# Output weights' lower parts on another engine, sums in pieces, loads spread over slots, and part of the first batch's keys and values among the preparation

## The chip, the cores and the metric

The kernel runs on one core of a Trainium2 chip. The metric is the time of one execution on the device in microseconds, median of several runs. In the profile the engines are PE (TensorE), PEld (its weight loads), DVE (VectorE), ACT (ScalarE), POOL (GpSimd) and SP (SyncE, which here issues every DMA).

## What is computed

Two attention layers over x and a context, both (32, 128, 1024) in float32, outputs the same shape. Cut to what matters:

```python
# layer 0, per batch: 8 heads of 16 rows, attention among the rows
q = Wq @ y + bq;  k = Wk @ y + bk;  v = Wv @ x + bv
attn = softmax(q k^T / sqrt(128))            # per head 16 x 16
o = Wo @ (attn v) + bo + x
h = norm_over_rows_and_columns(o) * gn_w[:, None] + gn_b[:, None]
# layer 1: 32 query heads of 32, 8 key heads, low-rank additions on every weight
lin(x, W, A, B) = x @ W + 2 * (x @ A @ B)
q = lin(h, Wq, Aq, Bq); k = lin(ctx, Wk, Ak, Bk); v = lin(ctx, Wv, Av, Bv)
attn = softmax(q k^T / sqrt(32))             # per head 128 x 128
out = h + lin(attn v, Wo, Ao, Bo)
```

## The kernel before

Every engine runs a program written out by hand; semaphores alone set the order between them, and each engine does its instructions strictly in its own order. Matrices are split in a rounded part and a rest ("hi" and "lo", type fp32r), and a product is three matmuls: hi x hi, hi x lo, lo x hi.

*Preparation.* The low-rank factors are merged into the key and value weights in eight units: `prep_product(n)` on TensorE, `prep_merge(n)` on VectorE, the high part on ScalarE, the low part on GpSimd (even n) or VectorE (odd n). `turn_layer0()` transposes the small weights of layer 0 behind unit 5.

*Batches.* For each of the 32 batches TensorE does the Gram matrix of y, the keys and values of layer 1 (`kv_products(b, chunks)`, eight chunks of 128 rows with three matmuls each, bank 2), and between these chunks the short chain of layer 0: `t1_product`, `score_product`, `n1_product`, `mix_product`, `mixed_x`. The result h goes to memory (h_dram). The output weights, merged with their factors, go to wo_dram as four blocks.

*Slots.* Then follows one loop over slots w = 0 to 511, the same on all engines. In slots 0 to 255 (QUERY_SLOTS is 256) TensorE projects queries, six matmuls a slot (`project_first`, `project_q`, L642); `split_q` on VectorE splits them, and `put_q` on SyncE writes them to q_dram every eight slots, 3 x 512 KB. `turn_h` transposes h in slots 0 to 26 and on, from h_in tiles that `load_h` brings. `scores(n)` (L697) takes a k_stack and a q_stack tile; VectorE makes their `maxima` and `negs` (L1190, L1195), ScalarE the `exponents` (L941), of which only the sums are kept. From slot 237 on one `scores_again(n)` a slot (L729) makes the scores a second time, transposed and with the logarithm of the sum subtracted, ScalarE makes the `probabilities` (probT, L958) and `context(k)` (L740) multiplies with the values.

In slots 256 to 511 TensorE projects the outputs: 16 pairs of batches of 16 slots each, with seven products per pair of 2x2 blocks in place of eight (`project_o`, L679). For these the four blocks of the output weights (w_blk, 1 MB each) are loaded by `load_wo` in the slots of WO_LOADS; GpSimd makes four differences of blocks (`out_weights`); ScalarE makes the high part of each of the seven weights in the slots of WO_PARTS (`out_hi`, L853), and GpSimd the low part (`out_lo`, L1458). Product m of pair 0 waits for `wo_lo` to reach m + 1. The weights' places are those of wq and hT, so each step also waits for a count of `q_mm`, the query projections done. VectorE splits the seven left operands (`split_op`, `combine`) and adds the products into the output blocks (`add_out`).

A score unit n has its slot in score_slot; its query load stands in slot 8 * queries_out + 10 at the earliest (score_load_at), its keys load in score_keys_at. again_load_at and again_rows_at place the loads of the second pass. SyncE works its slots in order too: a load that waits (for written queries in `wait_queries`, for a buffer) holds all behind it.

Order within a slot. TensorE: scores, product, transposes, context, scores_again. ScalarE: probabilities and context of the slot before, `keep_product`, `out_hi`, exponents. VectorE: maxima, transposed h, `split_q`, then from slot 256 the combinations, splits and sums.

## Time and profile before

| what | value |
|---|---|
| median of 3 runs | 1410.39 us (1408.95 to 1411.84) |
| the profiled execution's own time | 1413.77 us |
| its span, first to last instruction | 1412.0 us |
| mean granted clock of TensorE | 0.987 |
| busy: TensorE, VectorE, ScalarE, GpSimd | 1350.5, 935.0, 824.1, 190.4 us |
| exponents L941, mean of one | 343 ns, 1024 of them |
| probabilities L958, mean of one | 603 ns, 256 of them |
| high part of an output weight L853, mean of one | 1.9 us, 7 of them |

The page lists busy time per engine; waits are found in the views of waits and in the time lines, where a bracket behind a row gives the idle time before it and what ended it. Batches last from about 30 to 425 us, the query slots to 926.8 us, the pairs of output slots to the end.

### The profile page before, as it was taken

The numbers are of one execution on the slowest core, as the hardware profiler recorded it, in microseconds if no ns is written. First come the engines' busy times: TensorE is split into PE (matmuls) and PEld (weight loads), VectorE is DVE, ScalarE is ACT, GpSimd is POOL, SyncE is SP. The second block draws the span as 40 slices with busy tenths as digits, with TensorE's granted clock in tenths as the row PEclk, the third lists the DMA queues.
The fourth block names the chain that finished last, engine by engine and source line by source line (L and its number), as shares of the span: only waits on it lengthen the run. The fifth ranks groups of instructions, "written<-read, shape, count | busy, mean of one in ns | idle before, by whom it ended". The sixth has DMA issues, their size and how long they took to land.

```text
span 1412.0 us, 24026 instructions
## 1 busy us (share of the span) xinstructions
PE 1350.5 (96%) x7135; PEld 1062.1 (75%) x7135; DVE 935.0 (66%) x2061; ACT 824.1 (58%) x2924; POOL 190.4 (13%) x124
## 2 busy tenths in 40 slices
PE   6999999999989999999999997979999999999998
PEld 5777788787778788888888886656776676676666
DVE  5666666666555577777777774586766777766665
ACT  4556665555530677777757774556666666665440
POOL 5533332222210000000000002650000000000000
PEclk9999999999999999999999999999999999999999
DMA  6455556666747688888888889876988889877762
GB/s 177 143 196 202 201 200 203 224 220 224 249 151 225 226 260 266 258 254 263 254 252 262 253 253 289 249 224 200 250 248 246 255 250 253 250 228 229 229 216 75
DMA packets 220419, 321.42 MB, mean 228 GB/s; under 512 B 27586, under 2 KB 119332, under 8 KB 219780
## 3 DMA queue, kind: packets, MB, share of 16 engines
q1 hardware_dynamic: 220292, 319.88, 73.7%
q8 instruction: 61, 1.00, 0.3%
q14 instruction: 66, 0.54, 0.1%
HBM read 213.88 MB, written 105.91 MB: 226 GB/s over the span
## 4 chain that ended last, share of the span: by engine, by line
PE 80%; ACT 5%; DVE 5%; DMA 4%; issue 3%; SPq 2%; ACTq 0%; DVEq 0%
PE bank L642 23%; PE bank L679 21%; PE bank L538 10%; PE bank L697 7%; PE bank L729 5%; PE bank L740 4%; PE bank L613 2%; PE bank L488 2%; ACT lora_aT_kv L880 2%; DMA w_raw<-in_L_xattn_Wo 1%; DVE negs L1195 1%; SPq L1596 1%; DMA k_stack<-k_dram 1%; PE bank L563 1%; ACT x_hi L872 1%
## 5 line engine op out<-in xcount | busy, mean ns | idle before, releaser
L941 ACT ACTIVATE bank<-bank,negs 128x128 f32<-128x128 f32 x1024 | 348.8, 343 | 224.3 <-DVE negs L1195 224.1
L642 PE MATMUL bank<-hT,wq 128*128 128x512 f32 x1488 | 396.6, 404 | 3.1 <-DVE hT L1155 3.1
L679 PE MATMUL bank<-wo,op 128*128 128x512 f32 x1344 | 349.9, 398 | 2.0 <-DVE h_blk L1269 2.0
L642 PEld LDWEIGHTS bank<-hT,wq 128*128 128x128 f32 x1488 | 267.6, 191 | 51.3 <-DVE hT L1155 4.1
L679 PEld LDWEIGHTS bank<-wo,op 128*128 128x128 f32 x1344 | 252.1, 191 | 54.8 <-DVE op L1240 2.4
L1190 DVE TENSOR_REDUCE maxes<-bank 128x4 f32<-128x512 f32 x256 | 175.7, 686 | 146.8 <-PE bank L697 142.0
L958 ACT ACTIVATE probT<-bank 128x512 f32<-128x512 f32 x256 | 151.1, 603 | 106.2 <-PE bank L729 103.8
L941 ACT ACTIVATION_READ_ACCUMULATOR bank<-bank,negs 128x1 f32 x1024 | 212.7, 208 | 0.0
L538 PE MATMUL bank<-wkv_hi,yT 128*128 128x512 f32 x512 | 206.7, 425 | 0.0
L697 PEld LDWEIGHTS bank<-k_stack,q_stack 96*128 96x128 f32 x1024 | 151.5, 192 | 23.7 <-DMA k_stack<-k_dram 7.9
L697 PE MATMUL bank<-k_stack,q_stack 96*128 96x128 f32 x1024 | 148.8, 268 | 7.1 <-DMA k_stack<-k_dram 7.1
L729 PE MATMUL bank<-q_stack,k_stack 98*128 98x512 f32 x256 | 110.3, 432 | 15.3 <-ACT probT L958 15.3
L729 PEld LDWEIGHTS bank<-q_stack,k_stack 98*128 98x128 f32 x256 | 48.6, 190 | 82.2 <-ACT probT L958 39.3
L538 PEld LDWEIGHTS bank<-wkv_hi,yT 128*128 128x128 f32 x512 | 99.1, 193 | 14.3 <-issue 0.2
L1504 POOL TENSOR_TENSOR x_lo<-x_in,x_hi 128x1024 fp32r<-128x1024 f32 x32 | 76.2, 2383 | 236.7 <-ACT x_hi L872 236.7
L538 PE MATMUL bank<-wkv_lo,yT 128*128 128x512 f32 x256 | 101.5, 397 | 0.0
L1269 DVE TENSOR_TENSOR h_blk<-bank,h_blk 128x512 f32<-128x512 f32 x80 | 53.6, 687 | 71.6 <-PE bank L679 71.6
L832 ACT CAST yT<-bank 128x512 fp32r<-128x512 f32 x64 | 37.1, 581 | 108.2 <-PE bank L488 108.2
L1195 DVE TENSOR_SCALAR negs<-maxes 128x4 f32<-128x4 f32 x256 | 62.3, 243 | 27.3 <-DVE maxes L1190 0.5
L1240 DVE TENSOR_TENSOR op<-c_sb,op 128x512 fp32r<-128x512 f32 x96 | 70.7, 737 | 3.3
L740 PE MATMUL bank<-probT,v_in 128*32 128x512 f32 x512 | 68.2, 604 | 0.2
L1467 POOL TENSOR_TENSOR w_sum<-w_blk,w_blk 128x2048 f32<-128x2048 f32 x1 | 4.5, 4523 | 446.5 <-DMA w_blk<-wo_dram 446.5
(168 smaller groups left out, 1691.6 us busy)
## 6 DMA issues: line engine op xcount, KB each, us to landing
q_stack<-q_dram SPq DMA_DIRECT2D x512, 192.0 KB, 4.3
q_dram<-q_part SPq DMA_DIRECT2D x96, 512.0 KB, 4.1
k_stack<-k_dram SPq DMA_DIRECT2D x128, 192.0 KB, 4.3
y_in<-in_ctx SPq DMA_DIRECT2D x32, 512.0 KB, 4.2
x_in<-in_x SPq DMA_DIRECT2D x32, 512.0 KB, 4.9
h_dram<-h_out SPq DMA_DIRECT2D x32, 512.0 KB, 3.9
h_in<-h_dram SPq DMA_DIRECT2D x32, 512.0 KB, 3.8
h_blk<-h_dram SPq DMA_DIRECT2D x64, 256.0 KB, 4.9
```

Source lines behind the costliest of these rows:

```text
L538: m = pe.matmul(bank(2), yT[b % 2][:, c, part, :], w[:, c, :], start=first, stop=c == NC - 1 and part == 1)
L642: m = pe.matmul(bank(u % 2).rearrange("p (a n) -> p a n", a=2), wq[:, block, part, c, :], hT[(group + 1) % 2][:, :, of, c, :], start=c == ...
L679: mm = pe.matmul(out_bank(pair, m), op[m][:, of, c, :], wo[m][w][:, c, :], start=c == 0 and of == 0 and w == 0, stop=c == GROUP - 1 and of ...
L697: m = pe.matmul(score_bank(n)[:, j * P:(j + 1) * P], q_stack[place // GQ][SCORE_ROWS, g, j, :], k_stack[SCORE_ROWS, k % 2, g, :], start=Tr ...
L729: pe.matmul(again_bank(n), k_stack[STACK_ROWS, 2 + k % 2, g, :], again_stack(k)[STACK_ROWS, g, :, :].rearrange("p j n -> p (j n)"), start= ...
L740: m = pe.matmul(bank(3)[g * HD:(g + 1) * HD, :], v_in[:, k % 2, g, :], probT[:, (GQ * k + g) % PROBS, :], start=True, stop=True)
L941: act.activation(part, part, ACT.Exp, bias=negs[:, n % RING, j:j + 1], scale=SCORE1, accum_out=sums[:, score_column(k), g, j:j + 1]).then_ ...
L958: act.activation(probT[:, n % PROBS, :], again_bank(n), ACT.Exp, scale=SCORE1).then_inc(S["st_exp"], 1)
L1190: dve.tensor_reduce(largest, score_bank(n).rearrange("p (j t) -> p j t", j=GROUP), AX_X, ALU.max).then_inc(S["max"], 1)
L1195: dve.tensor_scalar(negs[:, n % RING, :], largest, -SCORE1, None, ALU.mult).then_inc(S["neg"], 1)
L1240: dve.tensor_tensor(op_part(m, 1), tile, f32(op_part(m, 0)), ALU.subtract).then_inc(S["op_lo"], 1)
L1504: pool.tensor_tensor(x_lo[:], x_in[b % 2][:], f32(x_hi[:]), ALU.subtract).then_inc(S["x_lo"], 1)
```

## The change

The lower parts of the seven output weights are made on VectorE, in halves of 128x1024, in slots given by the new table WO_LOWER; `project_o` of pair 0 waits for two counts per product. GpSimd makes the four differences only, each in four pieces of 128x512. The blocks are loaded in slots 227, 229, 232, 236 (before: 225, 227, 229, 231), and the high parts are made in slots 232, 246, 250, 254, 258, 260, 262 (before 230, 245, 249, 253, 257, 259, 261). Query loads stand at +12 in place of +10: the first eight go from slot 18 to slot 20, and those of units 16 to 18, 32 to 34 and so on up to 130 two slots, or one, later. The first eight loads of the second pass go from slots 224 to 227 (two each) to slots 229 to 236 (one each), its first two rows loads from slot 224 to 231 and 235. In batch 0 the chunks 0 to 4 of keys and values stand among the preparation, chunk n - 3 at the end of its step n.

```diff
--- before.py
+++ after.py
@@ -425,14 +425,18 @@
             return (NC * (b // GB) + GROUP * q + GROUP) // 2 - 1
 
 
-        WO_LOADS = {LAST_TURN + 1 + 2 * n: i for n, i in enumerate((0, 1, 2, 3))}
-        WO_PARTS = {QUERY_SLOTS + w: m for m, w in enumerate((-26, -11, -7, -3, 1, 3, 5))}
+        WO_LOADS = {QUERY_SLOTS + w: i for i, w in enumerate((-29, -27, -24, -20))}
+        WO_PARTS = {QUERY_SLOTS + w: m for m, w in enumerate((-24, -10, -6, -2, 2, 4, 6))}
+        WO_LOWER = {}
+        for m, halves in enumerate(((-18, -17), (-8, -7), (-4, -3), (-1, -1), (6, 7), (8, 9), (10, 11))):
+            for half, w in enumerate(halves):
+                WO_LOWER.setdefault(QUERY_SLOTS + w, []).append((m, half))
 
 
         score_load_at, score_keys_at, again_load_at, again_rows_at = {}, {}, {}, {}
         soonest = 0
         for n in range(SCORE_UNITS):
-            soonest = max(soonest, 8 * queries_out(score_half(n)) + 10)
+            soonest = max(soonest, 8 * queries_out(score_half(n)) + 12)
             if place_freed[n]:
                 soonest = max(soonest, score_slot[place_freed[n] - 1] + 1)
             score_load_at.setdefault(soonest, []).append(n)
@@ -441,10 +445,10 @@
 
         soonest = score_slot[TWO_STACKS - 1] + 1
         for n in range(HALVES * GQ):
-            again_load_at.setdefault(again_slot(n - 2 * GQ) + 1 if n >= 2 * GQ else soonest + n // 2, []).append(n)
+            again_load_at.setdefault(again_slot(n - 2 * GQ) + 1 if n >= 2 * GQ else max(soonest, again_slot(n) - 8), []).append(n)
         for k in range(HALVES):
             chunk = [k // (GB * NQ) in groups for groups in LOG_GROUPS].index(True)
-            soonest = max(soonest, log_slot[chunk] + LOG_OUT + 1, again_slot(GQ * (k - 1) - 1) + 1 if k >= 2 else 0)
+            soonest = max(soonest, log_slot[chunk] + LOG_OUT + 1, again_slot(GQ * (k - 1) - 1) + 1 if k >= 2 else again_slot(GQ * k) - 6)
             again_rows_at.setdefault(soonest, []).append(k)
 
         def score_column(k):
@@ -526,8 +530,13 @@
                                   start=c == 0, stop=c == NC - 1)
                 m.then_inc(S["gram_mm"], 1)
 
-            def kv_products(b, chunks):
+
+            EARLY = NC - 3
+
+            def kv_products(b, chunks, early=False):
                 for c in chunks:
+                    if b == 0 and early != (c < EARLY):
+                        continue
                     if c == 0 and b:
                         pe.wait_ge(S["kv"], b)
                     if b == 0:
@@ -651,7 +660,7 @@
                 if part == 0:
                     pe.wait_ge(S["op_lo"], PRODUCTS * pair + m + 1)
                     if pair == 0:
-                        pe.wait_ge(S["wo_lo"], m + 1)
+                        pe.wait_ge(S["wo_lo"], 2 * (m + 1))
 
                     if m == 0:
                         if pair:
@@ -751,6 +760,8 @@
                     gram_products(0)
                 if n == 4:
                     turn_layer0()
+                if n >= 3:
+                    kv_products(0, (n - 3,), early=True)
             for b in range(B):
                 if b:
                     gram_products(b)
@@ -1215,6 +1226,16 @@
                 dve.tensor_scalar(hi.bitcast(F32R), rows, 1.0, None, ALU.mult).then_inc(S["lse_hi"], 1)
                 dve.wait_ge(S["lse_hi"], chunk + 1)
                 dve.tensor_tensor(lo.bitcast(F32R), rows, hi, ALU.subtract).then_inc(S["lse_lo"], 1)
+
+            def out_lo(m, half):
+
+                of = slice(2 * half, 2 * half + 2)
+                if half == 0:
+
+                    dve.wait_ge(S["wo_mix"], (1, 4, 4, 3, 2, 3, 4)[m])
+                    dve.wait_ge(S["wo_hi"], m + 1)
+                dve.tensor_tensor(wo[m][1][:, of, :], wo_raw[m][:, of, :], f32(wo[m][0][:, of, :]),
+                                  ALU.subtract).then_inc(S["wo_lo"], 1)
 
             def split_op(pair, m):
 
@@ -1395,6 +1416,8 @@
                 chunk = log_chunk(w, LOG_ROWS)
                 if chunk is not None:
                     log_split(chunk)
+                for part in WO_LOWER.get(w, ()):
+                    out_lo(*part)
                 pair, i = step_of(w)
                 if pair > 0 and i == 0:
                     add_out(pair - 1, 11)
@@ -1452,33 +1475,29 @@
                 pool.wait_ge(S["prep_hi"], n + 1)
                 pool.tensor_tensor(lo, raw, f32(hi), ALU.subtract).then_inc(S["wkv_lo_pool" if n < FIRST_Q else "prep_lo"], 1)
 
-            def out_lo(m):
-
-                pool.wait_ge(S["wo_hi"], m + 1)
-                pool.tensor_tensor(wo[m][1][:], wo_raw[m][:], f32(wo[m][0][:]), ALU.subtract).then_inc(S["wo_lo"], 1)
+            def out_sum(made, a, b):
+
+                for c in range(GROUP):
+                    done = pool.tensor_tensor(made[:, c, :], a[:, c, :], b[:, c, :], ALU.subtract)
+                done.then_inc(S["wo_mix"], 1)
 
             def out_weights():
-                b11, b12, b22, b21 = (w_blk[i][:] for i in range(4))
-                t1, t2, last = (w_sum[m][:] for m in (3, 2, 6))
+                b11, b12, b22, b21 = w_blk
                 used = NC * (NG - 1)
+
                 for i in range(2):
                     pool.wait_ge(S[f"wo_in{i}"], DMA)
                 pool.wait_ge(S["q_mm"], used + 2)
-                pool.tensor_tensor(t1, b12, b11, ALU.subtract).then_inc(S["wo_mix"], 1)
+                out_sum(w_sum[3], b12, b11)
+                pool.wait_ge(S["wo_in2"], DMA)
                 pool.wait_ge(S["wo_mix"], 1)
-                out_lo(0)
-
-                pool.wait_ge(S["wo_in2"], DMA)
-                pool.tensor_tensor(b12, b22, b12, ALU.subtract).then_inc(S["wo_mix"], 1)
+                out_sum(b12, b22, b12)
                 pool.wait_ge(S["q_mm"], used + 3)
-                pool.tensor_tensor(t2, b22, t1, ALU.subtract).then_inc(S["wo_mix"], 1)
+                out_sum(w_sum[2], b22, w_sum[3])
                 pool.wait_ge(S["wo_in3"], DMA)
                 pool.wait_ge(S["q_mm"], used + 4)
                 pool.wait_ge(S["wo_mix"], 3)
-                pool.tensor_tensor(last, b21, t2, ALU.subtract).then_inc(S["wo_mix"], 1)
-                pool.wait_ge(S["wo_mix"], 4)
-                for m in range(1, PRODUCTS):
-                    out_lo(m)
+                out_sum(w_sum[6], b21, w_sum[2])
 
             def power(b):
                 pool.wait_ge(S["ve"], b + 1)
```

## Rows read from the trace of the kernel before

**Rows 1.** Windows: length, busy time (count) by engine, clock, DMA share, GB/s

```profile
462.00:469.00 7.00, 6.98 (x25) 6.01 (x26) 3.00 (x6) 2.27 (x13) 0.00 (x0) 0.57 0.69 243
...
853.31:883.13 29.82, 23.65 (x105) 19.51 (x105) 11.66 (x21) 12.36 (x46) 9.09 (x3) 0.89 1.01 320
883.13:926.80 43.67, 40.46 (x192) 29.11 (x191) 22.08 (x26) 25.79 (x73) 25.92 (x7) 0.96 0.85 249
926.80:972.72 45.92, 34.31 (x154) 23.46 (x152) 35.28 (x42) 25.38 (x72) 15.59 (x4) 0.89 0.63 187
972.72:1002.96 30.24, 30.24 (x154) 21.23 (x152) 21.19 (x40) 18.82 (x61) 0.00 (x0) 1.00 0.90 260
```

**Rows 2.** Waits of TensorE, 850 to 960: total, times, longest

```profile
PE bank L729 <- ACT probT L958: 14.7, 4, 7.3
PE bank L697 <- DMA k_stack<-k_dram: 6.2, 1, 6.2
```

**Rows 3.** Waits of TensorE, 440 to 470

```profile
PE bank L613 <- DMA h_in<-h_dram: 4.3, 1, 4.3
```

**Rows 4.** Time line of TensorE: start, length, line, [idle before, releaser]

```profile
462.02 1.09 PE L613 MATMUL bank<-ident,h_in 128*128 128x128 f32 x4 [4.26 <-DMA h_in<-h_dram]
...
463.66 2.87 PE L642 MATMUL bank<-hT,wq 128*128 128x512 f32 x6
```

**Rows 5.** Time line of TensorE around 900

```profile
898.25 0.56 PE L697 MATMUL bank<-k_stack,q_stack 96*128 96x128 f32 x4
898.65 1.60 PE L642 MATMUL bank<-hT,wq 128*128 128x512 f32 x6
...
900.32 1.56 PE L642 MATMUL bank<-hT,wq 128*128 128x512 f32 x6
...
901.96 1.57 PE L642 MATMUL bank<-hT,wq 128*128 128x512 f32 x6
```

**Rows 6.** VectorE's groups, 1002 to 1063: busy us, mean ns

```profile
L1240 DVE TENSOR_TENSOR op<-c_sb,op 128x512 fp32r<-128x512 f32 x12 | 8.3, 693 | 0.4
...
L1195 DVE TENSOR_SCALAR negs<-maxes 128x4 f32<-128x4 f32 x10 | 1.7, 170 | 1.1
```

**Rows 7.** Time line of VectorE, two of its negs

```profile
884.13 3.60 DVE L1195 TENSOR_SCALAR negs<-maxes 128x4 f32<-128x4 f32 x1
...
926.14 2.20 DVE L1195 TENSOR_SCALAR negs<-maxes 128x4 f32<-128x4 f32 x1
```

**Rows 8.** Time line of GpSimd

```profile
883.10 4.61 POOL L1472 TENSOR_TENSOR w_blk<-w_blk,w_blk 128x2048 f32<-128x2048 f32 x1
```

**Rows 9.** Time line of SyncE's queue, first slots

```profile
451.41 3.58 SPq L1643 DMA_DIRECT2D q_stack<-q_dram  x8
455.09 0.85 SPq L1602 DMA_DIRECT2D h_in<-h_dram  x2
```

**Rows 10.** Time line of SyncE's queue, slots 224 and on

```profile
854.61 2.02 SPq L1612 DMA_DIRECT2D q_dram<-q_part  x3
...
863.33 0.43 SPq L1628 DMA_DIRECT2D k_stack<-k_dram  x1
```

**Rows 11.** Landing of the k_stack loads issued in 860 to 890

```profile
DMA to landing us min/median/max: 6.7/9.0/11.2
```

**Rows 12.** GpSimd's groups, whole span

```profile
L1453 POOL TENSOR_TENSOR wq<-w_raw,wq 128x512 fp32r<-128x512 f32 x16 | 20.4, 1274 | 7.3 <-ACT wq L843 7.3
```

**Rows 13.** Time line of VectorE, first batch

```profile
24.02 0.28 DVE L1077 TENSOR_TENSOR gram<-bank,gram 128x128 f32<-128x128 f32 x1
```

**Rows 14.** Time line of TensorE, first batch

```profile
20.57 0.63 PE L538 MATMUL bank<-wkv_hi,yT 128*128 128x512 f32 x1
21.00 0.63 PE L538 MATMUL bank<-wkv_lo,yT 128*128 128x512 f32 x1
...
24.45 0.76 PE L563 MATMUL bank<-w0T,gram 128*128 128x128 f32 x2 [0.90 <-DVE gram L1077]
```

**Rows 15.** Landing of the w_blk loads

```profile
DMA to landing us min/median/max: 8.5/12.4/16.8
```

## Prediction, made before the changed kernel ran

> **What bounds the kernel now.** The page has TensorE busy for 96% of the span. I read windows of it first, then its waits, then the time lines around them. The second pair of output steps, 972.72 to 1002.96, is 30.24 us with no idle time; the first pair, with the same 154 matmuls, takes 45.92 us, **15.7 us more** [rows 1]. So time can only be won where TensorE waits, and the waits are few. In 850 to 960 us it waits 14.7 us for ScalarE's probT, four times, and once 6.2 us for a keys load; in 440 to 470 us once 4.3 us for h_in [rows 2, 3]. After a long wait the matmuls run slow: the six of a slot take 2.87 us against 1.56 [rows 4, 5], with the granted clock at a mean of 0.57, so partly at its lower level of 1.2 GHz [rows 1]. So each long wait costs itself and some 3 us behind it.
>
> Behind the probT waits stands GpSimd. VectorE's `negs` of four columns takes 0.17 us in quiet slots [rows 6]. The one of 884.13 took 3.60 us: it began inside a 128x2048 subtraction of GpSimd (883.10, 4.61 us) and ended with it, at 887.7 [rows 7, 8]. ScalarE waits for `negs` in its order, its probabilities stand behind, TensorE's `scores_again` two steps on behind these.
>
> The Trainium skill ("SBUF — State Buffer", Who interferes with whom) says that a VectorE instruction with two SBUF inputs, or in a two-port mode, and a GpSimd one that reads SBUF block each other for the whole of the earlier. By that rule the moved lower parts (two SBUF inputs) can be held by the sums too, once per piece; this case's trace agrees for `negs`. If both halves that fall among the sums were held so, it would take 2.6 us of VectorE's idle time and leave the sum as it is.
>
> **Prices of a slot.** From the six matmuls of one slot to those of the next are 1.64 us with a `scores_again` (900.32 to 901.96); the four score matmuls add 0.40 (898.25 to 898.65) [rows 5]. The second pair, 30.24 us, has 14 such slots, two without a product (0.24 each) and 5 scores, so a context is a quarter of the 4.8 left, 1.2. Without `scores_again` a slot is 1.4.
>
> **Part 1, score loads two slots later (+12).** In slot 18 SyncE issues two keys loads, then waits for the queries written in slot 17, and only at 451.41 goes on to eight query loads; `load_h(7)` and `load_h(8)` stand behind, at 455.09. `turn_h` of slot 24 waits for that load until 462.02 [rows 3, 4, 9]. With the block in slot 20, `load_h(7)` of slot 19 goes out once the transposes of slot 18 are done (six slots ahead of 457.8, so at about 448), 10 us ahead of its use. The query loads still go out when the queries are in memory, at about 451.4. What goes is 4.26 us of wait, and the slow stretch behind it: in 462 to 469 work of 0.36 (transposes) + 2 x (0.40 + 1.43) = 4.0 us took 7.0, so 2.9. Together 7.2. The 512 KB load now stands ahead of the first queries; bounds of that are 0 and 1.5 us (512 KB at 320 GB/s [rows 1] are 1.6), I take 0.3: **-6.9 us**. For the other groups nothing changes, since SyncE waited for the same writes at +10.
>
> **Part 2, loads spread (slots 224 to 255).** Slots 224 to 236 last 853.31 to 883.13 = 29.8 us; 13 x 1.43 + 6 scores x 0.40 + the log turn 0.3 = 21.3, so 8.5 are lost: the 6.2 of wait, and slow matmuls behind. The 20 slots behind, 883.13 to 926.80, last 43.67 us; 20 x 1.64 + 6 x 0.40 + 4 x 1.2 = 40.0, so 3.7 are lost, probT waits again. The keys load of 863.33 stands behind six query loads and two 1 MB blocks of the output weights, and lands 11.2 us later, while the DMA engines are full (share 1.01, 320 GB/s) [rows 1, 10, 11]. In the change only block 0 (slot 227) and the query writes of slot 225 stand ahead of it: 1.57 + 1.05 + 0.6 MB from 854.6 [rows 10] at 0.32 MB/us lands at about 865, before its use in slot 234 (about 869). This wait goes. But the bytes stay. Up to what `scores_again(4)` of slot 241 needs (`load_rows(1)`, behind the writes of slot 233 and block 2) 9.8 MB are issued: 30.6 us, that is 885.2, against an unhindered slot 241 at about 883. I leave 1.9 us for that (0 to 5), and 0.5 for slow matmuls. The probT waits of slots 237 to 255 go with GpSimd's long instructions (part 3). 8.5 + 3.7 - 2.4: **-9.8 us** (-5 to -12).
>
> **Part 3, lower parts on VectorE, sums in pieces.** GpSimd loses seven instructions of 4.6 us and keeps four sums of four 128x512 pieces. A 128x512 subtraction of its own took 1.27 us [rows 12]; so `negs` waits 1.3 us at most, in slots 232 to 243 only. In the trace the `negs` of 926.14, 2.0 us late, was followed by no wait of TensorE, and that of 884.13, 3.4 us late, by the shortest but one of the four waits, 1.8 us [rows 2, 7]. So the pieces cost nothing by themselves. VectorE gains 14 halves of 128x1024. A subtraction of 512 columns takes it 0.69 us, one of 128 columns 0.28, so 1024 take 0.69 + 512/384 x 0.41 = 1.2 us, 16.8 in all [rows 6, 13]. In slots 238 to 253 this lies in idle time (22.1 of 43.7 us are busy there [rows 1]).
>
> In the first pair it does not fit. In slots 255 to 267 TensorE needs 13 x 1.64 - 1.4 (slot 262 has no product) + 5 x 0.40 + 3 x 1.2 = 25.5 us. VectorE has 5 maxima with negs (0.85), `split_q` 1.4, 7 splits of op (1.07), 4 combinations (0.70), 9 sums (0.61) = 21.5 us, and now 8 halves, 9.6: 31.1 us. I walk the queues from slot 255 = 0: maxima 203, two halves, `split_q(63)`, two combinations and a split hold VectorE until 7.8, so the maxima of slot 257, ready at 4.2, are 3.6 late. ScalarE then does 1.4 of exponents, a probability, `keep_product`, the high part of product 4 (1.9 us, now slot 258). TensorE's `scores_again` waits 0.6 in slot 259, 1.2 in 260, its context 1.15 in 262 for the probabilities behind the high part of product 5, and product 4 in slot 265 waits 0.55 for its lower part. Sum 3.5 us in place of 15.7. The cover is thin: the lower parts of products 4 to 6 are made two slots ahead of their use, and every wait of TensorE here is one on VectorE's queue. With 1.2 for matmuls that run slow behind such gaps (bounds 0 and 2 x 1.3): **15.7 - 4.7 = -11.0 us** (-6 to -14).
>
> **Part 4, first batch's keys and values.** Five chunks, 15 matmuls, move ahead of two `prep_product`s. At that time one takes 0.43 us (20.57 to 21.00), a chunk 1.3 [rows 14]. Chunk 1 now stands ahead of prep 6 and chunk 2 ahead of prep 7; the merge of 7 comes 2 x 1.3 = 2.6 us later, less 0.3 that VectorE's own order held it back. With it go ScalarE's last high part and `sum_y(0)`, VectorE's `finish_gram(0)` (24.02) and the `t1` product, which waited for that until 24.45 [rows 13, 14]: +2.3. In return `score_product(0)` no longer stands behind chunk 2, which held it 0.6. The chunks 3 and 4 lay beside the softmax and give nothing. TensorE is not the bound there. **+1.7 us**; bounds: if the clock rises to 2.4 GHz within these chunks, matmuls take half, the delay halves and later ones gain about 1.3: -0.3; at most +2.8, two chunks and GpSimd's stacking of LoRA factors pushed past its use.
>
> Sum: -6.9 - 9.8 - 11.0 + 1.7 = -26.0 us. The profiled execution took 1413.8 (span 1412.0), so it would take 1387.8; the median of the runs is 1410.4 and goes to **1384.4 us**.
>
> **Rivals.** (a) VectorE becomes the bound in the first pair for more than I walked: its queue is 5.6 us over, and if all of it and a stretch at the low clock (3 us as behind 462) come through, 8.6 stay in place of 4.7, and one slot more of delay in splits makes it 10: +5, 1389.5. For it: the crowded slots 262 to 267; against: 9 us of its idle time in the second pair to catch up [rows 1]. Chance 0.18. (b) The DMA engines bound slots 224 to 241: nothing but order changes, and the backlog shows as a wait for rows or queries of 5 to 8 us with slow matmuls behind: 1384.4 + 6 = 1390.5. For it share 1.01; chance 0.12. (c) The pieces let nothing in between, GpSimd takes the port again at once: then `negs` of slots 234 to 243 are held up to 4 x 1.3 us, three waits of 1.4 to 1.8: 1384.4 + 5 = 1389.4. Against: the `negs` of 884.13 ended at 887.7, between two GpSimd instructions with no idle time between them [rows 7, 8]. Chance 0.05. (d) Slower: VectorE waits in its order. `out_lo(1, 0)` in slot 248 waits for the fourth sum, that for block 3 (issued in slot 236; a block took 8.5 to 16.8 us to landing [rows 15]) and GpSimd's three sums before. While VectorE stands there, maxima, splits and lower parts stand behind. It becomes a loss if the fourth sum ends more than 26 + 2 us after slot 248 (896), so later than 924; I have it at 894. At 930 it would give 1416. Chance 0.03. (e) The load order does nothing and the shift of the first batch and small waits eat the rest, within 0.2% of now: 1409, chance 0.02.
>
> **How the numbers follow.** My case 0.60, (a) 0.18, (b) 0.12, (c) 0.05, (d) 0.03, (e) 0.02. My case alone ranges 1379 to 1390 from its bounds. With (a) to (c), which may come together, the range is **1377 to 1397**. 0.2% (2.8 us) is about what a measurement of this kernel tells from no change. Faster 0.95, within 0.2% 0.02, slower 0.03.
>
> **What would show it.** Part 1: no wait of TensorE for h_in and full clock at 457 to 470. Part 2: no keys wait in slot 234; a wait of 0 to 5 us for DMA near slot 241. Part 3: `negs` never above 1.5 us; the first pair near 35 us, with several waits for probT of about 1 us. Part 4: `t1` at about 26.7 in place of 24.45, mixed_x(0) at 36.4 in place of 34.75. I am wrong if the first pair stays over 40 us, if a new wait over 3 us stands in 860 to 900, or if SyncE's queue delays a load in a stretch that was even.

## The result and the profile after

The changed kernel takes a median of **1391.15 us** (1388.16 to 1391.53, 4 runs) against 1411.12 (1408.95 to 1412.16) for the kernel before in the same measurement: ratio 0.9856, 95% interval 0.9837 to 0.9874. Measured again beside the experiments it gave 0.9854 (0.9832 to 0.9876). The forecast was 1384.4 (1377 to 1397): the sign and the range were right, but only two of its four parts were. In both measurements the medians differ by 20 us, where the forecast had 26.

The profiled execution has a span of 1389.7 us against 1412.0. Windows of it: length, busy time (count) of TensorE, its weight loads, VectorE, ScalarE and GpSimd, clock, DMA share, GB/s. The four later ones are slots 224 to 236, 237 to 255, the first and the second pair of output steps, and answer to [rows 1].

```profile
457.00:462.00 5.00, 5.00 (x32) 4.36 (x31) 3.70 (x8) 3.83 (x21) 0.00 (x0) 1.00 1.05 352
843.05:863.86 20.81, 20.81 (x105) 17.56 (x105) 10.74 (x21) 12.47 (x46) 1.48 (x2) 1.00 0.93 281
863.86:916.13 52.27, 42.63 (x192) 29.49 (x192) 23.93 (x33) 26.72 (x76) 18.62 (x15) 0.90 0.97 280
916.13:950.48 34.35, 31.16 (x153) 21.18 (x152) 30.09 (x49) 24.25 (x71) 0.00 (x0) 1.00 0.86 250
950.48:980.72 30.24, 30.24 (x154) 21.25 (x152) 21.18 (x40) 19.00 (x62) 0.00 (x0) 1.00 0.98 267
```

Side by side with before:

| stretch | before, us | after, us | difference | forecast |
|---|---|---|---|---|
| start to the first scores of slot 24 | 455.76 | 453.00 | -2.8 | +1.7 (part 4) |
| from there to `scores(3)` | 13.56 | 6.38 | -7.2 | -6.9 (part 1) |
| slots 224 to 236 | 29.82 | 20.81 | -9.0 | -8.5 |
| slots 237 to 255 | 43.67 | 52.27 | +8.6 | -3.7 + 2.4 |
| first pair | 45.92 | 34.35 | -11.6 | -11.0 (part 3) |
| all the rest | 823.3 | 822.9 | -0.4 | 0 |

The first row is one execution against one, and can't be put down to the change. Up to slot 18 the kernel of the first experiment below is the kernel before, and it got to the scores of slot 24 at 450.83. The eight profiled executions that share the changed kernel's program up to there got to them at 453.00 to 456.92. The first pair is the opposite: it takes 34.32 to 34.36 us in all nine profiled executions with the lower parts on VectorE, and 45.6 to 46.0 in all four with the old placement.

TensorE's waits of the end of the query slots, 850 to 960, which answer to [rows 2] (total, times, longest), and the same waits in the time line (start, length, line, [idle before, releaser]):

```profile
PE bank L738 <- DMA q_stack<-lse_dram: 9.2, 2, 5.7
PE bank L738 <- ACT probT L969: 1.5, 2, 0.9
PE bank L688 <- issue: 0.9, 1, 0.9
PE bank L749 <- ACT probT L969: 0.8, 1, 0.8
...
878.80 0.77 PE L738 MATMUL bank<-q_stack,k_stack 98*128 98x512 f32 x1 [5.72 <-DMA q_stack<-lse_dram]
892.73 0.47 PE L738 MATMUL bank<-q_stack,k_stack 98*128 98x512 f32 x1 [3.45 <-DMA q_stack<-lse_dram]
924.80 0.50 PE L738 MATMUL bank<-q_stack,k_stack 98*128 98x512 f32 x1 [0.63 <-ACT probT L969]
927.57 0.50 PE L738 MATMUL bank<-q_stack,k_stack 98*128 98x512 f32 x1 [0.90 <-ACT probT L969]
```

Of 14.7 us of waits for probT 2.3 are left, and the keys wait of 6.2 is gone. New are two waits of `scores_again` for a rows load, 9.2 us together, in slots 241 and 245. They undo what was won in the slots before. The time line of SyncE's queue shows what stood ahead of the first; the last line is from the kernel before:

```profile
858.52 7.16 SPq L1631 DMA_DIRECT2D q_dram<-q_part  x3
...
871.05 0.30 SPq L1689 DMA_DIRECT2D q_stack<-lse_dram  x1
...
875.56 5.91 SPq L1631 DMA_DIRECT2D q_dram<-q_part  x3
...
868.07 9.41 SPq L1612 DMA_DIRECT2D q_dram<-q_part  x3
```

The three query writes of 858.52, those of slot 233, took SyncE 7.16 us to issue. The writes of slot 225 take 2.02 in the kernel before [rows 10]; those of slot 233 took 9.41 there, so this hold is not new, but no load that TensorE waited for stood right behind it. Now the rows load stands behind it: it was issued at 871.05, and TensorE went on at 878.80.

### The profile page after: what moved, and what is told of

It is laid out like the page before. It is cut to its first block, busy times and chain, and to the rows that moved or that the text cites. A ratio compares the mean times of both kernels' runs of the same rounds, so it can differ in the third digit from the quotient of the medians.

```text
span 1389.7 us, 24051 instructions
## 1 busy us (share of the span) xinstructions
PE 1339.7 (96%) x7135; PEld 1052.9 (76%) x7135; DVE 928.3 (67%) x2075; ACT 824.0 (59%) x2924; POOL 160.1 (12%) x129
## 4 chain that ended last, share of the span: by engine, by line
PE 82%; ACT 6%; DMA 4%; DVE 4%; issue 3%; SPq 2%; ACTq 0%; DVEq 0%
PE bank L651 23%; PE bank L688 21%; PE bank L547 10%; PE bank L706 7%; PE bank L738 5%; PE bank L749 5%; PE bank L622 2%; PE bank L492 2%; ACT lora_aT_kv L891 2%; DMA w_raw<-in_L_xattn_Wo 1%; DMA q_stack<-lse_dram 1%; ACT x_hi L883 1%; PE bank L572 1%; ACT kv_sb L926 1%; PE bank L577 1%
## 5 line engine op out<-in xcount | busy, mean ns | idle before, releaser
L1261 DVE TENSOR_TENSOR op<-c_sb,op 128x512 fp32r<-128x512 f32 x96 | 67.4, 702 | 3.3
L1206 DVE TENSOR_SCALAR negs<-maxes 128x4 f32<-128x4 f32 x256 | 44.7, 175 | 27.3 <-DVE maxes L1201 0.5
L1066 DVE TENSOR_TENSOR yT<-bank,yT 128x512 fp32r<-128x512 f32 x64 | 43.8, 686 | 24.5 <-ACT yT L843 24.5
```

The costliest lines, as they stand in the source:

```text
L1261: dve.tensor_tensor(op_part(m, 1), tile, f32(op_part(m, 0)), ALU.subtract).then_inc(S["op_lo"], 1)
```

## Experiments

Each is measured against the kernel before on the same chip in the same measurement.

### The query loads two slots later, alone

```diff
-            soonest = max(soonest, 8 * queries_out(score_half(n)) + 10)
+            soonest = max(soonest, 8 * queries_out(score_half(n)) + 12)
```

> The kernel before with +12 in place of +10 for the query loads, nothing else. My theory (a load of h stood behind the query loads of slot 18): TensorE's wait for h_in of 4.3 us and the slow matmuls behind it go, about -7 us, 1404 against 1411. Rival: the first query loads now stand behind that load and the wait only moves to the first scores; then within 0.2% of before.

Measured: 1402.21 us against 1411.19, ratio 0.9935 (0.991 to 0.996). Right. TensorE has no wait in 440 to 470 and its clock is 1.00 there; a 512 KB load ahead of the queries cost nothing that can be seen. From the scores of slot 24 to `scores(3)` the profiled execution takes 6.30 us in place of 13.56.

```profile
457.00:462.00 5.00, 5.00 (x31) 4.37 (x30) 3.91 (x8) 3.77 (x22) 0.00 (x0) 1.00 1.07 355
```

### The early chunks alone

```diff
+                if n >= 3:
+                    kv_products(0, (n - 3,), early=True)
```

> The kernel before with the five chunks of keys and values of batch 0 among the preparation, nothing else. Theory of the prediction: the chunks stand ahead of the last two merges and delay the chain, +1.7 us. Theory from the changed kernel's trace: TensorE reaches its full clock some 10 us sooner (matmuls of 0.23 us apart from about 17 us on in place of 27), batch 0 ends 4.5 us sooner, and 1.6 us of it are left from batch 2 on: -1.6 us in the run's time.

Measured: 1410.67, ratio 0.9998 (0.9984 to 1.0011), no difference. The time line of TensorE shows two things that work against each other:

```profile
21.30 0.39 PE L543 MATMUL bank<-wkv_lo,yT 128*128 128x512 f32 x1
21.52 0.39 PE L543 MATMUL bank<-wkv_hi,yT 128*128 128x512 f32 x1
...
23.74 0.46 PE L568 MATMUL bank<-w0T,gram 128*128 128x128 f32 x2 [1.71 <-DVE gram L1084]
...
25.73 1.92 PE L488 MATMUL bank<-ident,y_in 128*128 128x128 f32 x8
27.30 0.78 PE L543 MATMUL bank<-wkv_hi,yT 128*128 128x512 f32 x1
```

In the kernel before, matmuls of 512 columns follow each other at 0.43 us (20.57 to 21.00, [rows 14]) until 28 us. Here they run at 0.22 to 0.23 (21.30 to 21.52) from about 16.5 us on: TensorE is at 2.4 GHz in place of 1.2 some 11 us earlier. (The clock column of the windows says 1.00 for 16 to 31 us of the kernel before and 0.89 here, the other way round; here the spacing tells the level.) But then it has nothing to do for 1.71 us, and 2 us on it runs slow again (0.57 from 27.30 to 27.87). The first x_lo product starts at 32.27 in place of 35.30, that of batch 2 at 62.47 in place of 62.62.

But this start moves by itself as well. The kernel of the first experiment has none of these chunks and the same program here as the kernel before; in its profiled execution the spacing is down to 0.23 by 23 us and not at 28, and the first x_lo product starts 4.2 us earlier (first line, the kernel before; second line, the first experiment):

```profile
35.30 0.62 PE L598 MATMUL bank<-x_lo,mix_split 128*128 128x512 f32 x2
...
31.12 0.62 PE L598 MATMUL bank<-x_lo,mix_split 128*128 128x512 f32 x2
```

So of the start only this is shown: in all twelve profiled executions with fifteen matmuls more in the preparation the full pace is there by 17 us, and in the two without it came at 23 and 28. How long it then lasts varies too. Behind the waits of 1.7 and 0.6 us it was lost in six of the nine executions with moved chunks, this one among them, and kept in three, one of them the changed kernel's first.

### Extra matmuls in those places, the chunks left in the batch

```diff
+                if n >= 3:
+                    c = n - 3
+                    for part, w in ((0, wkv_hi), (0, wkv_lo), (1, wkv_hi)):
+                        pe.matmul(bank(2), yT[0][:, c, part, :], w[:, c, :], start=True, stop=True)
```

> The kernel before with 15 more matmuls in the preparation at the places of the moved chunks (each product overwritten later); the batch keeps all its own chunks, so the output is that of before. If the earlier clock is what gains in batch 0, mixed_x(0) comes at 31 to 32.5 us in place of 34.8 although no work left the batch. If it was the work moved out of the batch, the 15 only stand in the way: 34.8 or later, up to 36.5, and the run's time is the same or 1 to 2 us longer.

Measured: 1408.66, ratio 0.9974 (0.9958 to 0.9991), faster by 2.5 us with fifteen matmuls more to do.

```profile
23.75 0.46 PE L563 MATMUL bank<-w0T,gram 128*128 128x128 f32 x2 [0.32 <-DVE gram L1083]
...
31.68 0.63 PE L598 MATMUL bank<-x_lo,mix_split 128*128 128x512 f32 x2
```

The chunks now fill the hole ahead of `t1` (0.32 us of wait in place of 1.71), the full pace holds from 16 to 31 us, and x_lo is 3.6 us early in batch 0 and still 2.3 in batch 3. No work left the batch, so an early x_lo needs no moved work. That the fifteen matmuls gain by the clock is likely and not shown: without them the first experiment's execution was 4.2 us early in batch 0 and 2.8 in batch 3. Nor is it shown that moving work gives nothing, since the changed kernel's x_lo (30.83) came before this one's.

### The loads of slots 224 to 236 back where they were

The changed kernel without part 2:

```diff
-        WO_LOADS = {QUERY_SLOTS + w: i for i, w in enumerate((-29, -27, -24, -20))}
+        WO_LOADS = {LAST_TURN + 1 + 2 * n: i for n, i in enumerate((0, 1, 2, 3))}
-            ... else max(soonest, again_slot(n) - 8), []).append(n)
+            ... else soonest + n // 2, []).append(n)
-            ... if k >= 2 else again_slot(GQ * k) - 6)
+            ... if k >= 2 else 0)
```

> The changed kernel with the block loads in slots 225, 227, 229, 231, the first eight loads of the second pass in slots 224 to 227 and their rows in slot 224, as before; all other parts of the change stay. If spreading the loads is worth the 9.8 us of the prediction, this takes 1401. If the bytes ahead of slot 241 bind in any order, the 9.2 us of waits for rows at slots 241 and 245 turn into one of about 6 in slot 234 with slow matmuls behind: 1391, within 2 us of the changed kernel.

Measured: 1384.77 (1382.30 to 1388.85), ratio 0.9807 (0.9784 to 0.983). This is **better than the changed kernel**, whose intervals begin at 0.9837 and 0.9832. Part 2 does not help. By the ratios it costs some 7 us, and some 4 by the later version with extra matmuls (0.9825). Its cost can't be read from the trace: the profiled execution, 1388.85, is the slowest of the five. Of the two forecasts the second is the nearer: a wait for keys in slot 234 took the place of those for rows, of 8.97 us and not 6. But the median is 6 us under what it said.

### The changed kernel again

> The changed kernel once more, beside the next three on the same chip: 1389 to 1393 against 1411 of the kernel before. Its trace shows whether the two waits for rows (5.7 us in slot 241, 3.5 in slot 245) come back in another execution or wander.

Measured: 1387.98 (1386.66 to 1391.79) against 1408.13, ratio 0.9854 (0.9832 to 0.9876), as at first. Its two waits for rows are 5.57 and 3.30 us, so they come back. Its profiled execution (1391.79) is the slowest of its five.

### Two megabytes more, and the rows first

Two runs on what binds slots 224 to 256. In the first, two copies of 1 MB within DRAM stand behind the loads of blocks 0 and 1:

```diff
                 sp.dma_start(w_blk[i][:], wo_dram[i]).then_inc(S[f"wo_in{i}"], DMA)
+                if i < 2:
+                    sp.dma_start(spare[i], wo_dram[i]).then_inc(S["spare"], DMA)
```

> The changed kernel with two more copies of 1 MB (memory to memory, read by nobody), issued right behind block loads 0 and 1. Theory 'bytes': between slots 224 and 256 the DMA engines have no room, every MB costs its time at 0.31 MB/us; 2.1 MB more are 6.8 us longer, 1398, with the rows waits grown to about 16 us. Rival 'order and latency' (a small load stands behind a few large ones, with room elsewhere): two issues more cost under 2 us of SyncE's time and the total moves by less than 3 us.

Measured: 1392.95 against 1387.98 for the changed kernel beside it, +5.0. But only 0.5 us of it lies in slots 224 to 255 of the profiled execution (72.3 against 71.8), and of the 2.7 us between the two profiled executions 2.5 lie ahead of slot 24, before any copy. The copies were cheap, so they were a poor probe: in 860 to 865 the window has 462 GB/s at a DMA share of 1.23, against 297 at 1.07 in the changed kernel beside it. In these windows a byte of such a copy took less of the DMA engines' time than one of the other traffic.

```profile
860.00:865.00 5.00, 4.99 (x24) 3.94 (x23) 2.23 (x4) 3.50 (x12) 0.00 (x0) 1.00 1.23 462
```

In the second, `load_rows(1)` stands three slots earlier, the query writes stand behind the other loads of their slots, and blocks 2 and 3 two slots later:

```diff
-            ... if k >= 2 else again_slot(GQ * k) - 6)
+            ... if k >= 2 else again_slot(GQ * k) - 9)
-        WO_LOADS = {QUERY_SLOTS + w: i for i, w in enumerate((-29, -27, -24, -20))}
+        WO_LOADS = {QUERY_SLOTS + w: i for i, w in enumerate((-29, -27, -22, -18))}
```

> The changed kernel with rows 1 loaded in slot 232 in place of 235, the query writes of slots 241, 249 and 257 issued behind the loads of their slot, and blocks 2 and 3 in slots 234 and 238 in place of 232 and 236. By 'order' both waits for rows (9.2 us, with slow matmuls behind some 12) go: 1380. By 'bytes' the wait only goes to another load of the same stretch; what is gained is what the blocks leave to slots after 241, up to 3 us: 1388 to 1391.

Measured: 1386.4, ratio 0.9841 (0.9817 to 0.9865), 1.6 us under the changed kernel beside it, within the noise. In the profiled execution slots 224 to 255 take 66.1 us against 71.8. The wait in slot 241 is gone and the other grows from 3.3 us:

```profile
886.97 0.76 PE L738 MATMUL bank<-q_stack,k_stack 98*128 98x512 f32 x1 [4.91 <-DMA q_stack<-lse_dram]
```

### Fewer query writes

In the changed kernel the writes of rows 1 and 2 of the last five write slots go out for one batch in four; the rest of those rows is filled by copies in slots 169 to 201. The queries concerned are not the true ones.

```diff
-                    sp.dma_start(halves[:, row, :, :], f32(q_part[pair % 2][:, part, :, :, :]).rearrange(
+                    bs = slice(0, 1) if row and pair >= 27 else slice(None)
+                    sp.dma_start(halves[:, row, bs, :], f32(q_part[pair % 2][:, part, bs, :, :]).rearrange(
```

> The changed kernel, but of the query writes of the last five write slots (225, 233, 241, 249, 257) the rows 1 and 2 go out for one batch of four only; the other three quarters of those rows are filled by copies within DRAM eight pairs back, issued in slots 169 to 201 (so the queries of these pairs are not the true ones). It takes about 0.79 MB out of each of the five writes. If slots 224 to 256 are bound by what the DMA engines have to move (share above 1.0 from 850 to 895), up to slot 241 1.6 to 2.4 MB less are ahead of the rows load: 5 to 7 us at 0.32 MB/us. Both waits for the rows (5.7 and 3.5 us) go or leave under 1 us, slot 224 to 256 goes from 73 or 72 us to 62 to 64, and the time from 1388 to about 1379 (ratio 0.979). If it is the place of the rows load in SyncE's order, or its wait for the logarithms, the waits stay at over 4 us in sum and the time moves by less than 3 us.

Measured: 1384.83, ratio 0.9823 (0.9805 to 0.9841). The stretch does as the first theory said, the time does not (it had 1379):

```profile
847.95:911.30 63.35, 60.83 (x293) 46.22 (x294) 35.27 (x54) 39.18 (x122) 21.89 (x16) 0.97 0.92 278
...
887.93 0.47 PE L738 MATMUL bank<-q_stack,k_stack 98*128 98x512 f32 x1 [2.52 <-DMA q_stack<-lse_dram]
```

Slots 224 to 255 take 63.35 us in place of 71.8, the wait in slot 241 is gone and 2.52 of the other are left. The whole gained only half of that: in this execution slot 224 starts at 847.95 against 844.47, 2.1 of it already late at slot 24 (before anything was changed) and 1.0 in waits for keys behind the copies. Without a wait the stretch takes 59.3 us: 20.81, as measured for slots 224 to 236, and 38.5 of work behind them (the window of 870.75 below). So 4 us are left of 12.5, and most of what is lost there comes with the query writes. The run does not tell apart the two ways in which they act, since both went: the bytes that the DMA engines move, and SyncE's hold. The writes of slot 233 took SyncE 1.45 us to issue in place of 6.65, and the rows load of slot 235 went out 20.6 us behind the first product of slot 224 in place of 27.5. The DMA share stayed above 1.0 from 860 to 890, with a wait of 2.52 us only.

### The sums in one piece each

```diff
-                for c in range(GROUP):
-                    done = pool.tensor_tensor(made[:, c, :], a[:, c, :], b[:, c, :], ALU.subtract)
+                done = pool.tensor_tensor(made[:], a[:], b[:], ALU.subtract)
```

> The changed kernel with each of GpSimd's four sums as one 128x2048 instruction in place of four pieces; the lower parts stay on VectorE. If it is the length of one GpSimd instruction that holds VectorE, negs or a split in slots 232 to 245 takes up to 4.6 us; but TensorE waits for rows there anyway, so it costs 0 to 3 us: 1391 to 1394. If pieces let nothing in between, there is no difference in any negs.

Measured: 1389.74, ratio 0.9859 (0.9838 to 0.9879): no difference. VectorE's `negs` are held again, and nobody minds:

```profile
870.05 4.57 POOL L1480 TENSOR_TENSOR w_blk<-w_blk,w_blk 128x2048 f32<-128x2048 f32 x1 [3.25 <-DMA w_blk<-wo_dram]
...
870.64 4.00 DVE L1206 TENSOR_SCALAR negs<-maxes 128x4 f32<-128x4 f32 x1
...
884.66 3.70 DVE L1206 TENSOR_SCALAR negs<-maxes 128x4 f32<-128x4 f32 x1
...
914.89:949.24 34.35, 31.13 (x153) 21.18 (x152) 30.09 (x49) 24.25 (x71) 0.00 (x0) 1.00 0.86 246
```

In both cases TensorE stands for the rows then or from then on (5.48 us up to 878.37, 3.02 up to 891.50), so that the late `negs` delays nothing that can be seen: slots 224 to 255 take 71.7 us against 71.8. So this run doesn't say what the pieces are worth without these waits.

### The lower parts back on GpSimd, in pieces

```diff
+            def out_lo(m):
+                pool.wait_ge(S["wo_hi"], m + 1)
+                for c in range(GROUP):
+                    done = pool.tensor_tensor(wo[m][1][:, c, :], wo_raw[m][:, c, :], f32(wo[m][0][:, c, :]), ALU.subtract)
+                done.then_inc(S["wo_lo"], 1)
```

> The changed kernel, with the seven lower parts back on GpSimd, each in four pieces of 128x512. My theory: what cost 15.7 us in the first pair of output steps was the length of a hold on VectorE (up to 4.6 us), not the work itself, so pieces of 1.2 to 1.3 us each are enough and moving the work to VectorE gains little. VectorE then has 8.5 us less to do in slots 255 to 267, so the four waits there (3.2 us in sum) shrink or go, but pieces run beside it and hold single instructions for up to 1.3 us each: negs up to 1.3 us, first pair 32 to 36 us, time 1384 to 1389, that is within 3 us of the changed kernel's 1388. The rival, that the lower parts had to leave GpSimd: four pieces back to back hold VectorE as one long instruction does, negs of over 3 us, first pair over 40 us, time 1394 to 1400.

Measured: 1393.45, ratio 0.9885 (0.9866 to 0.9905). By the ratios that is some 4 us over the changed kernel, with intervals that overlap; I had said at most 3. Neither theory had it right. The first pair takes 37.56 us: much less than the 45.92 of before with whole instructions, more than 34.35.

```profile
917.90:955.46 37.56, 32.63 (x154) 22.08 (x153) 29.75 (x41) 24.89 (x71) 22.14 (x15) 0.95 0.81 230
...
928.55 12.86 POOL L1479 TENSOR_TENSOR wo<-w_blk,wo 128x512 fp32r<-128x512 f32 x8 [7.01 <-ACT wo L864]
...
L1261 DVE TENSOR_TENSOR op<-c_sb,op 128x512 fp32r<-128x512 f32 x14 | 14.5, 1034 | 0.5
...
938.64 0.50 PE L738 MATMUL bank<-q_stack,k_stack 98*128 98x512 f32 x1 [2.93 <-ACT probT L969]
```

The longest `negs` in 855 to 965 is 1.25 us, as the forecast of the mechanism had it. But VectorE's lower parts of op, with two SBUF inputs, take 1.03 us on average, in place of 0.76 in the changed kernel (same window, 830 to 980) and 0.69 in quiet slots [rows 6], and GpSimd's eight pieces take 1.6 us each in place of 1.27 [rows 12]. VectorE is busy for 29.75 us without the eight halves (9.8 us) that are in the 30.09 of the changed kernel. So in the first pair both placements load VectorE alike, once with the work, once with being held.

### Two candidates

The version with the loads back, and the one with the rows first, each with the fifteen extra matmuls in place of the early chunks.

```diff
+                if n >= 3:
+                    c = n - 3
+                    for part, w in ((0, wkv_hi), (0, wkv_lo), (1, wkv_hi)):
+                        pe.matmul(bank(2), yT[0][:, c, part, :], w[:, c, :], start=True, stop=True)
-                if n >= 3:
-                    kv_products(0, (n - 3,), early=True)
```

> The changed kernel with the loads of slots 224 to 236 back where they were (which gave 0.9807) and the first batch's chunks back in the batch, with 15 extra matmuls without a use in their places among the preparation. In the kernel before the extra matmuls gave 0.9974 against 0.9998 for the moved chunks. If both gains add: ratio 0.978 to 0.980, about 1381, x_lo of the first batch near 31.7 with the clock at full from 16 to 31 us. If the moved chunks do as well here as the extra matmuls, the same as 0.9807.

Measured: 1384.95, ratio 0.9825 (0.9804 to 0.9846).

> The changed kernel with rows loads three slots earlier, the last query writes behind the other loads of their slots and blocks 2 and 3 in slots 234 and 238 (which took slots 224 to 256 from 71.8 to 66.1 us in the profiled execution, 0.9841 in median), and with the 15 extra matmuls in place of the moved chunks. If the order of the loads decides which wait comes, and the whole is bound by the DMA engines only up to slot 245: 224 to 256 in 66 us, one wait of 5 us for rows, time 1380 to 1384, ratio 0.978 to 0.981. If the 5.7 us of that profiled execution are given back behind it, as its median of 1386.4 against 1388.0 says, ratio 0.983 and no better than with the loads back.

Measured: 1386.57, ratio 0.9833 (0.9815 to 0.9851). Neither gives more than the loads back alone; the 2 us of the extra matmuls are not to be seen here. The first has an unexpected trace, though. Its loads of slots 224 to 236 are those of the version with the loads back, in the same order, and slot 224 starts within 0.4 us (843.82 and 843.46). The two programs differ in the first batch only. Waits of that version, then of this one:

```profile
868.42 1.08 PE L706 MATMUL bank<-k_stack,q_stack 96*128 96x128 f32 x4 [8.97 <-DMA k_stack<-k_dram]
```

```profile
862.87 1.09 PE L704 MATMUL bank<-k_stack,q_stack 96*128 96x128 f32 x4 [3.06 <-DMA k_stack<-k_dram]
```

and their windows of 850 to 870, in the same order:

```profile
850.00:870.00 20.00, 11.03 (x55) 9.17 (x54) 6.92 (x15) 7.92 (x33) 3.24 (x3) 0.82 0.99 264
```

```profile
850.00:870.00 20.00, 16.94 (x71) 13.78 (x71) 9.04 (x18) 9.33 (x41) 8.03 (x7) 0.83 1.03 357
```

With the DMA engines busy at a share of 1 in both, one execution moved 5.3 MB in these 20 us and the other 7.1. Slots 224 to 255 took 71.6 us in the one and 66.0 in the other. Slots 237 to 255 of the second are the nearest to that stretch without a wait (0.59 us in all, clock 1.00), and price its work, 38.5 us:

```profile
870.75:909.83 39.08, 38.49 (x191) 28.05 (x191) 23.55 (x33) 26.55 (x76) 13.19 (x9) 1.00 0.97 281
```

The length of that stretch in all profiled executions:

| kernel | slots 224 to 255, us |
|---|---|
| before | 73.5 |
| changed; measured again; sums whole | 73.1; 71.8; 71.7 |
| two megabytes more | 72.3 |
| loads back; loads back with extra matmuls | 71.6; 66.0 |
| rows first; rows first with extra matmuls | 66.1; 67.3 |
| lower parts on GpSimd in pieces | 72.4 |
| fewer query writes | 63.4 |
| without a wait, 20.8 + 38.5 | 59.3 |

## Why the prediction was right where it was, and wrong where it was not

**Part 1: right.** Forecast -6.9, measured -7.2 in the stretch (-7.3 with that edit alone), and -9.0 in median for that edit alone (-5.6 to -12.7 by its interval). Both terms held: 4.26 of wait and 2.9 of slow matmuls behind it. The bound of 0 to 1.5 for the load ahead of the queries came out at its lower end.

**Part 2: wrong, -0.4 in place of -9.8.** The keys wait of slot 234 went as forecast, and slots 224 to 236 took 20.81 us where I had priced 21.3. The step that failed is what I left for slots 237 to 255: 40.0 of work, 1.9 of wait near slot 241 and 0.5 of slow matmuls. The 40.0 is itself 1.5 too high: from 883.13 to 926.80 are 19 slots, 237 to 255, and not 20, and 38.5 is what the work takes. The stretch took 52.27, so 13.8 over the work: waits of 5.72 and 3.45, one of 0.47 for a bank, and 4.1 by which the matmuls ran slow (the clock is 0.90). Three terms were too small. The first wait by 3.8: the time at which TensorE gets to slot 241 was right (883 in the times of before; slot 224 starts 10.3 earlier now, and TensorE was there at 878.80 - 5.72 = 873.1), the landing of the rows was not. I had counted 9.8 MB at 0.32 MB/us. By the window below 10.6 MB had moved when the rows came; that the loads issued behind the rows load took the rest is likely, but no run shows it alone. The second wait I had not looked for at all, though what stood in the queue behind the first load was the same backlog, and the third term, the slow matmuls, came with these two.

```profile
845.00:878.80 33.80, 27.61 (x135) 22.62 (x134) 15.54 (x27) 15.82 (x62) 13.43 (x11) 0.97 1.04 315
```

This is near rival (b), to which I gave 0.12: nothing but order changes. The run with fewer writes bears out its premise (8.4 us less in the stretch with less to move), and the run with the loads back shows that the new order is no better. That no order helps is not shown: with the rows first the stretch took 66.1 and 67.3 us in two profiled executions, against 71.7 to 73.1 in the three with the changed kernel's order in the table's second row. The ratios moved by 2 to 3 us only, within their intervals, and one execution with the old order took 66.0 as well. The warning had been in the rows: a share of 1.01 over the stretch, and a keys load that landed late [rows 1, 11].

**Part 3: right.** -11.0 forecast, -11.6 measured. I had walked waits of 0.6, 1.2, 1.15 and 0.55 us in the first pair; the trace has 0.63, 0.90, 0.79 and 0.88. The prices held as well:

```profile
L1237 DVE TENSOR_TENSOR wo<-w_blk,wo 128x1024 fp32r<-128x1024 f32 x8 | 9.5, 1218 | 2.4 <-POOL w_sum L1481 2.4
L1237 DVE TENSOR_TENSOR wo<-w_sum,wo 128x1024 fp32r<-128x1024 f32 x6 | 7.1, 1220 | 0.0
...
L1206 DVE TENSOR_SCALAR negs<-maxes 128x4 f32<-128x4 f32 x29 | 6.2, 212 | 3.1
```

A half takes 1.22 us (forecast 1.2 from two smaller sizes). I had added 1.2 us for slow matmuls; the clock in the pair is 1.00. The longest `negs` was 0.84, below the bound of 1.5, so rival (c) is out; its reason, that VectorE gets in between two back-to-back GpSimd instructions, held. Rival (a), VectorE as the bound, is there as a tendency (30.09 of 34.35 us busy) and cost what was priced. The run with pieces on GpSimd shares out the gain: its first pair is 8.4 us shorter than before and 3.2 longer than the changed kernel's, so the larger part comes without moving the lower parts to VectorE. Whether the sums had to be cut is open, since TensorE waits for DMA when they run.

The Trainium skill ("SBUF — State Buffer", Who interferes with whom) says that a VectorE instruction with two SBUF inputs and a GpSimd one that reads SBUF exclude each other. The trace of the run with pieces on GpSimd agrees: 1034 ns in place of 760 in the same window of the changed kernel, and GpSimd's pieces longer too.

**Part 4: wrong.** +1.7 forecast. The early chunks alone moved the median by nothing (-2.3 to +1.6 us by the interval). I had priced a chunk by TensorE's pace in the kernel before, 0.43 us a matmul, and given the rise to 2.4 GHz as a bound only. It came with the first chunk, and matmuls took half: `t1` started at 23.28, against 24.45 [rows 14] and a forecast of 26.7, and the first x_lo at 30.83 in place of 35.30. The 1.6 us that are left of this from batch 2 on, and the 2.8 at slot 24, are no larger than what the first experiment's execution had without any chunk moved (2.8 in batches 2 and 3, 4.9 at slot 24), so how much of them is this part's stays open. The step that failed is a price read at one level of the clock and used for a stretch in which the change itself moves the level.

**The total** came to -22.3 us in the profiled executions where I had -26.0: 9.4 too much in part 2, 4.5 too little in the start, 0.9 too little in parts 1 and 3, 0.4 elsewhere. By the medians it is -20.0. That the profiled sum came so near is luck: a start that varies by 4 to 5 us between executions of one program made up for half of the error of part 2. The median fell in the range of 1377 to 1397, and outside that of my own case, 1379 to 1390.

## What to carry to other kernels

When a wait stands behind DMA engines at a share of 1, don't count it as won by another order before the whole backlog has been followed to the next loads and the next slots, from the new start times; in these runs less to move in the full stretch took away 8.4 of 12.5 us. Long passes on GpSimd next to a VectorE with little slack are best given to VectorE, or else cut: the first pair went from 45.9 us to 37.6 by cutting and to 34.4 by moving. Cutting pays by less than the length of the hold suggests, since each piece still holds and is held. Price what is added to a thinly filled start of TensorE at both levels of the clock, and read the level from the spacing of the matmuls. Before a gain of a few us is read from one trace, look where an execution of the same program stands at that point.

## What was not expected of the hardware

Fifteen 512-column matmuls without a use, placed from 16 us on in gaps of TensorE, made the kernel faster (0.9974, 0.9958 to 0.9991). The pace went from 0.43 to 0.23 us a matmul by 17 us; in the two executions without them it did so at 23 and 28. A wait of 1.7 with one of 0.6 us behind it lost it again for about 3 us in six executions of nine, and did not in three.

With the same loads in the same order the DMA engines moved 264 GB/s in one execution and 357 in another, at shares of 0.99 and 1.03, and the stretch differed by 5.6 us while the two medians agree (1384.77 and 1384.95). This is larger than most differences between the kernels here, and one profiled execution can't tell two load orders apart. Here the DMA share said that the engines were busy and not how much they moved.

SyncE, which only issues, stood for 7.16 and 5.91 us in issuing three writes whose issue takes 2.02 in slot 225, for 9.41 in the kernel before and for 11.36 with the loads back. While it stood for the 7.16, the rows load behind it was not even issued.

```profile
859.05 11.36 SPq L1631 DMA_DIRECT2D q_dram<-q_part  x3
```
